# Transposing normalised rows by DMA instead of TensorE in a one-core vision layer

## The reference

```
patches = patchify(x)                          # 64 x 196 x 768
h = concat(cls, patches @ W_lin.T + b_lin)     # 64 x 197 x 192
h = h + attention(layernorm(h))                # 12 heads of 16, q and k normalised
y = layernorm(h)                               # the mixture part starts here
scores = sigmoid(y @ gate.T)                   # 8 experts in 4 groups
cw = weights of the best 2 experts in the best 2 groups, normalised; else 0
out = h + sum_e cw[e] * ((silu(y @ w1[e].T) * (y @ w3[e].T)) @ w2[e].T)
        + (silu(y @ sw1.T) * (y @ sw3.T)) @ sw2.T
```

## Time and profile before

| | us |
|---|---|
| median of 3 runs | 1838.97 |
| lowest, highest | 1836.14, 1839.57 |
| the profiled execution | 1838.55 |
| its span | 1836.8 |
| granted clock of TensorE, mean | 0.99 |

### The profile page before, as it was taken

One profiled execution on the slowest core, in us unless ns is written; L12 is line 12 of the kernel. 1 busy time (PEld: TensorE's weight loads), 2 busy tenths in 40 slices (PEclk: granted clock), 3 DMA queues, 4 the chain that ended last, 5 costly groups with the idle time before them and its releaser, 6 DMA issues. The chain is left out here.

```text
span 1836.8 us, 43648 instructions
## 1 busy us (share of the span) xinstructions
PE 1756.6 (96%) x16914; PEld 1218.7 (66%) x16914; DVE 1213.8 (66%) x3497; ACT 977.9 (53%) x2078; POOL 302.9 (16%) x338
## 2 busy tenths in 40 slices
PE   3899999999999999999999959999999999999998
PEld 2677777777777777777777635555555555555555
DVE  4555555555555555555555438888888888888887
ACT  2555555555555555555555534545454545545453
POOL 0000000000000000000000003443434343444433
PEclk9999999999999999999999979999999999999999
DMA  5011111111111111111111010001010101000000
GB/s 186 2 51 51 51 51 51 52 51 42 45 51 51 51 51 51 52 51 45 44 48 51 11 37 27 27 27 35 19 36 18 36 18 36 21 33 27 24 18 15
DMA packets 31641, 75.67 MB, mean 41 GB/s; under 512 B 3467, under 2 KB 16430, under 8 KB 31310
## 3 DMA queue, kind: packets, MB, share of 16 engines
q1 hardware_dynamic: 31438, 72.89, 12.7%
HBM read 53.51 MB, written 19.37 MB: 40 GB/s over the span
## 5 line engine op out<-in xcount | busy, mean ns | idle before, releaser
L585 ACT ACTIVATE prob<-ps_sc 99x792 f32<-99x792 f32 x384 | 317.3, 827 | 88.2 <-PE ps_sc L427 88.2
L1216 POOL TENSOR_TENSOR in_lo<-inner,in_hi 128x512 f16<-128x512 f32 (+1 forms) x225 | 257.9, 1146 | 433.2 <-ACT act L1003 432.9
L372 PE MATMUL ps_hid<-lin_f,xin 128*99 128x192 f32 x1536 | 283.8, 328 | 32.2 <-DMA xin<-xp 28.1
L372 PEld LDWEIGHTS ps_hid<-lin_f,xin 128*99 128x99 f32 x1536 | 239.4, 167 | 33.4 <-DMA xin<-xp 28.1
L1149 DVE SCALAR_TENSOR_TENSOR acc<-ps_y,comb,acc 128x192 f32<-128x192 f32 (+1 forms) x700 | 242.0, 408 | 0.3 <-PE ps_y L945 0.3
L1011 ACT ACTIVATE in_hi<-inner 128x512 f16<-128x512 f32 (+1 forms) x225 | 140.3, 623 | 181.4 <-DVE inner L1131 181.4
L1003 ACT ACTIVATE act<-ps_h 128x512 f32<-128x512 f32 (+1 forms) x225 | 131.7, 585 | 189.3 <-PE ps_h L929 189.3
L943 PE MATMUL ps_y<-w_hi,in_hi 128*128 128x192 f16 (+1 forms) x900 | 223.9, 249 | 4.1 <-DVE acc L1149 2.6
L1131 DVE SCALAR_TENSOR_TENSOR inner<-ps_h,act 128x512 f32<-128x512 f32 (+1 forms) x225 | 153.8, 684 | 102.9 <-ACT act L1003 99.3
L945 PE MATMUL ps_y<-w_hi,in_lo 128*128 128x192 f16 (+1 forms) x900 | 221.4, 246 | 0.0
L944 PE MATMUL ps_y<-w_lo,in_hi 128*128 128x192 f16 (+1 forms) x900 | 221.4, 246 | 0.0
(11 more groups left out here) (148 smaller groups left out, 3198.0 us busy)
## 6 DMA issues: line engine op xcount, KB each, us to landing
xin<-xp SPq DMA_DIRECT2D x64, 594.0 KB, 4.3
hidden_dram<-h SPq DMA_DIRECT2D x64, 147.0 KB
hin<-hidden_dram SPq DMA_DIRECT2D x24, 384.0 KB, 3.0
out<-acc SPq DMA_DIRECT2D x24, 384.0 KB, 2.3
w_f<-w SPq DMA_DIRECT2D x1, 2304.0 KB, 9.9
hidden_dram<-h SPq DMA_DIRECT2D x64, 0.8 KB
w_f<-w SPq DMA_DIRECT2D x1, 864.0 KB, 11.5
qkv_f<-w_qkv SPq DMA_DIRECT2D x1, 576.0 KB, 3.9
```

Source lines behind the costliest of these rows:

```text
L372: last = pe.matmul(hid[:, t, :], xin[q][:, k, t * TR:(t + 1) * TR], lin_f[:, k, :], start=(k == 0), stop=(k == PCHUNKS - 1))
L585: act.activation(prob[quad][:, places].rearrange("p h m s -> p h (m s)"), ps_sc[0:TR, places, 0:2 * SLOTS], ACT.Exp, scale=D ** -0.5 / (SQ ...
L1216: pool.tensor_tensor(in_lo[b][:, 0:N], inner[b][:, 0:N], in_hi[b][:, 0:N], ALU.subtract).then_inc(inlo_done, 1)
```

## The change

The rows are transposed by DMA. ScalarE normalises without the doubled columns (the scale now holds the factor 64, made by GpSimd), and makes `y_hi`, the float16 rounding, from the rows before they are transposed; VectorE makes `y_lo = bnorm - y_hi`. The doubled columns 192 to 255 are made in these two steps, by a second instruction each. SP then issues eight DMA transposes a group, four for each half, from y_hi and y_lo to `yT_hi` and `yT_lo`, each of 128 (or 80) rows by 256 float16. TensorE no longer transposes; its gate waits for the eight DMAs and stands after step 5 instead of 4, writing to a PSUM tile of its own. `gate_out` moves to step 5; on VectorE the subtractions stand in steps 1 and 2, the statistics in 3 and 4, and route parts 0 and 1 both in step 6. SP's order in a body is: transposes of half 0 of the following group, load, transposes of half 1, store. The diff, without the renamed semaphores and the hunks that only rename:

```
-        bnorm = sb("bnorm", [128, T, 256])
+        bnorm = sb("bnorm", [128, T, C])
+        y_hi = sb("y_hi", [128, T, 256], F16)
+        y_lo = sb("y_lo", [128, T, 256], F16)
...
-        ps_x = [ps(f"ps_x{k}", [128, 512]) for k in range(2)]
+        ps_gate = ps("ps_gate", [128, 512])
...
+            def transposes(g, half_no):
+                R, p = rows_of(g), g.mod(2)
+                sp.wait_ge(ylo_done, g.times(2, half_no + 1))
+                if half_no == 0 and reached(g.times(NE, -NE)):
+                    sp.wait_ge(inner_done, g.times(NE, -NE))
+                for t in (2 * half_no, 2 * half_no + 1):
+                    s = slice(t * R, (t + 1) * R)
+                    sp.dma_start_transpose(yT_hi[p][:, :, s], y_hi[0:R, t, :]).then_inc(yT_in[p], 16)
+                    sp.dma_start_transpose(yT_lo[p][:, :, s], y_lo[0:R, t, :]).then_inc(yT_in[p], 16)
+
+            first = Index(0, 0, 2, GROUPS_B)
             for g in range(3):
                 load(Index(0, g, 2, GROUPS_B))
+            transposes(first, 0)
+            transposes(first, 1)
 
             def body(g):
+                following = g.back(-1)
+                if following.active():
+                    transposes(following, 0)
                 if g.back(-3).active():
                     load(g.back(-3))
+                if following.active():
+                    transposes(following, 1)
                 store(g)
...
-            def transposes(g):
-                R = rows_of(g)
-                pe.wait_ge(bnorm_done, g.times(2, 2))
+            def gate(g):
+                R, p = rows_of(g), g.mod(2)
+                pe.wait_ge(yT_in[p], g.halves(32 * T, 32 * T))
 
                 if reached(g.times(1)):
                     pe.wait_ge(tanh_done, g.times(1))
                 for t in range(T):
                     s = slice(t * R, (t + 1) * R)
-                    for k in range(2):
-                        last = pe.transpose(ps_x[k][:, s], bnorm[0:R, t, k * 128:(k + 1) * 128], id32[0:R, 0:R])
-                last.then_inc(yT_done, 1)
...
-                    if e == 2 and following.active():
-                        transposes(following)
-                    if e == 4 and following.active():
+                    if e == 5 and following.active():
                         gate(following)
...
+                ts = slice(2 * half_no, 2 * half_no + 2)
                 act.wait_ge(bneg_done, g.times(1, 1))
+                if reached(g.times(2, half_no - 1)):
+                    act.wait_ge(ylo_done, g.times(2, half_no - 1))
+                for t in (2 * half_no, 2 * half_no + 1):
+                    last = act.activation(bnorm[0:R, t, :], hin[p][0:R, t, :], ACT.Identity,
+                                          scale=brstd[0:R, t:t + 1], bias=bshift[0:R, t:t + 1])
+                last.then_inc(bnorm_done, 1)
+                act.wait_ge(bnorm_done, g.times(2, half_no + 1))
+
                 if half_no == 0 and reached(g.times(1)):
-                    act.wait_ge(yT_done, g.times(1))
-                for t in (2 * half_no, 2 * half_no + 1):
-                    for dst, src in ((slice(0, C), slice(0, C)), (slice(C, 256), slice(128, C))):
-                        last = act.activation(bnorm[0:R, t, dst], hin[p][0:R, t, src], ACT.Identity,
-                                              scale=brstd[0:R, t:t + 1], bias=bshift[0:R, t:t + 1])
-                last.then_inc(bnorm_done, 1)
...
+                    before = g.back(1)
+                    act.wait_ge(yT_in[before.mod(2)], before.halves(32 * T, 32 * T))
+                act.activation(y_hi[0:R, ts, 0:C], bnorm[0:R, ts, :], ACT.Copy)
+                act.activation(y_hi[0:R, ts, C:256], bnorm[0:R, ts, 128:C], ACT.Copy).then_inc(yhi_done, 1)
...
+            def rest_of(g, half_no):
+                R = rows_of(g)
+                ts = slice(2 * half_no, 2 * half_no + 2)
+                dve.wait_ge(yhi_done, g.times(2, half_no + 1))
+                dve.tensor_tensor(y_lo[0:R, ts, 0:C], bnorm[0:R, ts, :], y_hi[0:R, ts, 0:C], ALU.subtract)
+                dve.tensor_tensor(y_lo[0:R, ts, C:256], bnorm[0:R, ts, 128:C], y_hi[0:R, ts, C:256],
+                                  ALU.subtract).then_inc(ylo_done, 1)
...
-                    if e in (2, 4) and ahead.active():
-                        stats_of(ahead, e // 2 - 1)
-                    if e == 3 and following.active():
-                        yT_out(following)
-                    if e > 4 and following.active():
+                    if e in (1, 2) and following.active():
+                        rest_of(following, e - 1)
+                    if e in (3, 4) and ahead.active():
+                        stats_of(ahead, e - 3)
+                    if e == 6 and following.active():
+                        route(following, 0)
+                    if e > 5 and following.active():
                         route(following, e - 5)
...
-                pool.tensor_scalar(bvareps[0:R], bmv[0:R, :, 1], EPS, None, ALU.add).then_inc(bve_done, 1)
+                pool.tensor_scalar(bvareps[0:R], bmv[0:R, :, 1], EPS, 1.0 / SX ** 2,
+                                   ALU.add, ALU.mult).then_inc(bve_done, 1)
```

More of the change, by code:

```diff
@@ L770, in phase_b @@
 def phase_b(nc, hidden_dram, out, sem, sb, bufs):
-    w13_hi, w13_lo, w2_hi, w2_lo, gate_hi, gate_lo, id32, gbias, bef4, bef8, minus_half = (
-        bufs[n] for n in "w13_hi w13_lo w2_hi w2_lo gate_hi gate_lo id32 gbias bef4 bef8 minus_half".split())
+    w13_hi, w13_lo, w2_hi, w2_lo, gate_hi, gate_lo, gbias, bef4, bef8, minus_half = (
+        bufs[n] for n in "w13_hi w13_lo w2_hi w2_lo gate_hi gate_lo gbias bef4 bef8 minus_half".split())
     with ExitStack() as ctx:
@@ L816, in phase_b @@
         ps_y = [ps(f"ps_y{b}", [128, 512]) for b in range(2)]
-        ps_x = [ps(f"ps_x{k}", [128, 512]) for k in range(2)]
+        ps_gate = ps("ps_gate", [128, 512])
         h_in = [sem(f"h_in{p}") for p in range(3)]
+        yT_in = [sem(f"yT_in{p}") for p in range(2)]
         acc_out = [sem(f"acc_out{p}") for p in range(2)]
[L822 to L828, removed]
+        gate_done, inner_done, y_done = sem("gate_done"), sem("inner_done"), sem("y_done")
+        yhi_done, tanh_done, silu_done, inhi_done = (
+            sem("yhi_done"), sem("tanh_done"), sem("silu_done"), sem("inhi_done"))
+        bst_done, bmv_done, bnorm_done, ylo_done = (
+            sem("bst_done"), sem("bmv_done"), sem("bnorm_done"), sem("ylo_done"))
         route_step, route_done = sem("route_step"), sem("route_done")
@@ L892, in transposes @@
                     s = slice(t * R, (t + 1) * R)
-                    for k in range(2):
-                        last = pe.transpose(ps_x[k][:, s], bnorm[0:R, t, k * 128:(k + 1) * 128], id32[0:R, 0:R])
-                last.then_inc(yT_done, 1)
[L897 to L903, removed]
+                    dst = ps_gate[0:R, t * E:(t + 1) * E]
                     pe.matmul(dst, yT_hi[p][:, 0, s], gate_hi[:, 0], start=True, stop=False)
@@ L912, in inner_products @@
                 N, p, b = T * rows_of(g), g.mod(2), (g.c + e) % 2
-                if e == 0:
-                    pe.wait_ge(yThi_done, g.times(2, 2))
-                    pe.wait_ge(yTlo_done, g.times(2, 2))
                 if reached(g.times(NE, e - 1)):
@@ L948, in _ @@
             first = Index(0, 0, 2, GROUPS_B)
-            transposes(first)
             gate(first)
@@ L992, in gate_out @@
                 act.wait_ge(gate_done, g.times(1, 1))
-                act.activation(half[0:R], ps_x[0][0:R, 0:T * E].rearrange("p (t e) -> p t e", e=E), ACT.Tanh,
+                act.activation(half[0:R], ps_gate[0:R, 0:T * E].rearrange("p (t e) -> p t e", e=E), ACT.Tanh,
                                scale=0.5 / SS).then_inc(tanh_done, 1)
@@ L1015, in _ @@
             normalise(first, 1)
-            yT_out(first)
             gate_out(first)
@@ L1166, in _ @@
                 stats_of(second, half_no)
-            yT_out(first)
+            for half_no in range(2):
+                rest_of(first, half_no)
             for part_no in range(4):
```

7 lines of the change are left out of this document (removed).

## The result

The changed kernel takes 1933.4 us (1933.06 to 1935.23, 4 runs) against 1837.68 us (1836.14 to 1839.57, 4 runs): ratio 1.0522, 95% interval 1.0504 to 1.0541. It is 96 us slower, where 1832 us, 7 us faster, was forecast. 1933 lies inside the stated range, near its upper end (1935), but not for the reason that put the end there: that end stood for a pitch of 1.65 us, and the measured pitch, 1.29 us, gave 1874 us (rival 1). That it lies inside is luck.

What follows compares the result with a forecast made beforehand. TensorE, busy 96% of the span, was taken as the bound: -20.5 (transposes gone) + 10.8 (stalls) + 2.4 (lead-in) = -7.3 us on 1838.55 us, said as 1832 us; range 1819 to 1935 us.

Steps and rivals of the forecast that it cites:

- a pitch of 1.65 us: Queued transposes on SP at the range's upper end: 4.5 us over the window, 107 us, lead-in 9.7, 1935 us.
- rival 1: TensorE in front of the gate: transposes land late at t = 1.3, 48 us plus lead-in 7.2, 1874 us; chance 0.20.
- t = 0.6: SP queue: assumed pitch in us of queued transposes; last lands 6.5 us after the first issue, hidden with 3 us to spare.
- The window: From y_lo of the first half being ready to the gate: 9.4 us without stalls, 9.8 us with them.
- The point of decision: Pitch at which cover is gone and TensorE waits in front of the gate: (9.8 - 2.3) / 7 = 1.07 us.
- t = 0.32: SP queue: lowest pitch, as the issue of a plain DMA; with no stall -19.9 us, 1819 us.
- Gain of TensorE: Eight transposes gone from TensorE: 0.87 us a group, 20.5 us in all.
- Stalls of steps 2 to 4: TensorE waiting behind late silu/accumulate (0.15 us) and the port (0.3 us) a group: 10.8 us over 24 groups.
- The port: VectorE's second subtraction pair against GpSimd's in_lo of expert 2: bounds 0 and 0.6 us a group, 0.3 taken.
- Period with all stalls and no late DMA: One group of the mixture part: near 29.3 us, 28.8 without stalls, against 29.69 before.
- Lead-in: First group, nothing hides it: transposes 2.1 us later plus normalise 0.26, together +2.4 us.
- rival 2: TensorE in front of the gate: each transpose takes a whole landing, t = 2.3, +210 us, 2049 us; chance 0.09.

Runs made afterwards that it cites:

- experiments 6: Changed kernel, still eight transposes, each moving only the first 128 columns (32 KB instead of 64 KB) from the third group on: 1925.63 us, ratio 1.0476.
- experiment 3: Changed kernel with y_hi and y_lo side by side in one tile, four merged transposes of 128 KB a group instead of eight: 1829.54 us, ratio 0.9952.
- experiment 1: Changed kernel with the eight DMA transposes replaced by plain DMAs of the same 64 KB, rows arriving untransposed: 1830.35 us, ratio 0.9959.
- experiment 2: Changed kernel with the load of hin issued behind the transposes of half 1 instead of between the halves: 1918.09 us, ratio 1.0431.
- experiment 5: Kernel of experiment 3 with the two subtractions in the other order, the narrow one (128 columns) first: 1822.30 us, ratio 0.9916.
- experiment 4: Changed kernel, eight transposes, normalise one step earlier, subtractions ahead of route in steps 0 and 1, load behind the transposes: 1884.24 us, ratio 1.0248.

## Why the prediction was wrong

**The step that failed** is "I take t = 0.6, nearer the low end because issue and bytes both lie there". t was the pitch of queued transposes; it is 1.29 us (rows of the changed kernel above). The row by which it was priced was the issue of a plain DMA, 0.32 us, and the bytes of a store. Bytes don't enter: 1.23, 1.25, 1.27 us for 32, 64, 128 KB (experiments 6 and 3). A plain DMA between the same tiles is issued in 0.62, at a pitch near 0.65 (experiment 1), so the value was right for the operation that the trace of before held, and wrong for the one that the change adds. The window was right: with y_lo of half 0 at 1408.25 and the unstalled gate at 1421.61 - 3.71 = 1417.9 it was 9.65 us, against 9.4 (no stalls) to 9.8 (with them) worked out. The point of decision was a little off, since the load's issue stands in the same queue: (9.65 - 2.4 - 0.6) / 7 = 0.95 us and not 1.07, which changes nothing at 1.29.

**What lay under rival 1.** It gave 1874 us at t = 1.3, with the pitch almost as measured, and 1933 came. The difference is of three terms that its sum did not have: the load's issue inside the same queue (0.6 us a group, experiment 2: 14 us); long issues of 1.7 to 2.6 us, whose cause is open (0.4 us a group, 10 us); and the clock, which fell behind 19 of the 24 waits (some 30 us in all). The last was no part of any rival. 7 x 1.29 + 2.4 = 11.4 us, plus 0.6 and 0.4 is 12.4, less 9.65 gives 2.8; the mean wait is 2.9. So 1933 us inside the range confirms neither its end nor rival 1's sum: the mechanism of rival 1 was right, and these terms filled the rest by chance. One sum has a slip: at t = 0.32 the lead-in with both its terms comes to 0.3 us and not 0.6, which moves 1819 us by 0.3.

**What was right.** Gain of TensorE: 0.87 us a group; in experiment 5 the period is 28.93 us between two stores, against 28.8 worked out with no stalls. Stalls of steps 2 to 4: forecast 0.15 + 0.3, measured in experiment 3 as (3.20 - 3.15) + (3.52 - 3.15) + (3.22 - 3.15) = 0.49 us (first outer products at 1397.19, 1400.39, 1403.91, 1407.13). The port was given as a coin toss decided by 50 ns, and was one in the changed kernel: of the 22 narrow subtractions of half 1, 13 took 1.24 to 1.25 us and 9 took 0.28, and TensorE waited for accumulate in 13 of 22 groups. In experiment 3 in_lo won in all 22. The price was 0.37 us on TensorE and not 0.6. Experiment 5 shows the mechanism from the other side. Period with all stalls and no late DMA: forecast 29.3, in experiment 3 29.31 (stores at 1397.05 and 1426.36). Lead-in: forecast +2.1, at t = 1.3 +7.2; measured +6.8.

**The rule against the change** was that of the Trainium skill (VectorE: DVE Perf Modes, The three transpose paths): 1309 ns for a 128x128 transpose by DMA. The trace has a figure near it, 1.29 us from one issue to the next, but it belongs to something else: here it is the price of one instruction on SP for two squares, for four (experiment 3) or for one (experiment 6), while landing takes 2.4 us. Taken per instruction the figure gives t = 1.3 and rival 1, where the prediction had put it nearest to rival 2; taken per square it gave 2110 us. The other sentence of the Trainium skill (DMA: Bandwidth & Descriptors, Latency and other measured facts, 261 GB/s) speaks of bytes, which never bound here. What the Trainium skill says of the port (SBUF — State Buffer, Who interferes with whom) holds: in experiments 3 and 5 whichever started first kept the other out. That section of the Trainium skill also names tensor_scalar among the operations that can contend, as den does in experiment 4 (0.82 against 0.17 us). Taken strictly the rule gave 0.6 us a group; in_lo did win every time in experiment 3, and the price was 0.37.

## What to carry to other kernels

Price a DMA that moves off a busy engine as a queue: so many issues times what an issue of that very kind keeps its queue, plus everything else in that queue, against the window between the data being ready and the first reader. If no row shows that kind of issue, the kernel is decided by an unknown, and the number of instructions is the first thing to cut: eight transposes of 64 KB lost 96 us here, four of 128 KB won 9, and with two lines in another order 15.5. A wait on TensorE can cost more than its length, when the clock falls behind it. No run issued a part of the transposes from another engine, so nothing here says what a second queue would do.

## What the runs showed of the hardware

- The issue of a DMA transpose of 128 rows of float16 keeps SP 1.23 to 1.27 us (medians), for 32, 64 or 128 KB, and 1.28 us with nothing in flight before it; landing is 2.4 to 2.5 us after the issue starts. A plain DMA of 64 KB between SBUF tiles is issued in 0.62 us, back to back with others, and lands in 2.0. A plain DMA of 384 KB needs 0.32 to 0.34 alone and 0.57 to 0.58 behind transposes.
- Some issues of a transpose take 1.6 to 2.6 us. They recur with the count of transposes: every 9 to 13 (or two or three times that) with eight a group, every 16 with four a group in experiment 5, none in experiment 3.
- TensorE's clock stood at its lower level for 3.4 us behind 19 of the 24 waits of the changed kernel (0.95 over the group). The length of the wait alone doesn't decide it: it fell behind waits of 1.75 to 3.71 us and held behind five of 2.19 to 3.08 us. In experiment 2 it fell behind a wait of 1.75 us and held behind one of 2.88; in experiment 4 it fell behind four of 23, of 1.79 to 2.20 us, and held behind waits of 1.83 to 2.01.
- A fp32 operation of VectorE on four numbers a partition with one SBUF input (den, L1123) took 0.82 us on average beside GpSimd's in_lo in experiment 4, 0.17 us in the changed kernel, where in_lo doesn't run beside it; the reduction just before it (L1122, 0.19 us) was not held up by the same in_lo.
